# Cross-attention and mixture of experts on one Trainium2 core: attention over context rows as loaded, split products in it, and a new order of work up to the first expert

## What is computed

```
adj = layernorm(x)                       # 4 x 512 x 512, the "adjacency" of a graph attention layer
layer(h, W, a_self, a_neigh, b):         # 8 heads of 64
    feat  = h @ W[head]
    e     = leaky_relu(feat·a_self + (feat·a_neigh)^T, 0.2) - 1e10 * (1 - adj)
    out   = softmax(e) @ feat + b        # concatenated over heads, then elu
x = x + layer(layer(ctx, W0, ...), W1, ...)
xn = layernorm(x)
scores = sigmoid(xn @ router_w^T); top 3 of 8 groups, then top 4 of 32 experts; weights normed, times 2.5
each expert takes at most CAP = 80 tokens: its first ones, in the order of the tokens
x = x + sum over experts of w * (silu(xt @ W_gate) * (xt @ W_up)) @ W_down
      + (silu(xn @ shared_gate^T) * (xn @ shared_up^T)) @ shared_down^T
```

## Time and profile before

| | |
|---|---|
| median of 3 runs | 539.58 us (537.31 to 541.82) |
| span of the profiled execution, first to last instruction | 534.8 us |
| time of the profiled execution itself | not given apart from its span |
| PE matmul busy | 439.8 us, 82% |
| DVE busy | 270.0 us, 50% |
| ACT busy | 159.8 us, 30% |
| DMA | 85.55 MB, mean 160 GB/s |

### The profile page before, as it was taken

How to read it: one execution, slowest core, us unless ns; L and a number is a source line. 1 busy time by engine, 2 the same in 40 slices (tenths; PEclk the granted TensorE clock), 3 DMA queues, 4 the chain that set the end, 5 groups by cost and what they waited for, 6 DMA issues and landing times.

```text
span 534.8 us, 6440 instructions
## 1 busy us (share of the span) xinstructions
PE 439.8 (82%) x2363; PEld 339.8 (64%) x2363; DVE 270.0 (50%) x670; ACT 159.8 (30%) x275; POOL 127.0 (24%) x118
## 2 busy tenths in 40 slices
PE   0251687789958898997999999999999999999920
PEld 0221343334445576876789898888988898888810
DVE  5853638988975999667132243322334334332300
ACT  0222422433187301111112242333324233333220
POOL 0577200300000100000321233332234344332211
PEclk9997679999978999999975999999999999999985
DMA  8687060110126500000178977899979897977250
GB/s 260 162 178 208 25 237 0 79 78 1 80 81 237 198 10 11 0 2 0 39 135 258 277 212 235 249 286 288 319 225 321 256 303 241 307 249 224 28 91 12
DMA packets 41057, 85.55 MB, mean 160 GB/s; under 512 B 14496, under 2 KB 14496, under 8 KB 39488
## 3 DMA queue, kind: packets, MB, share of 16 engines
q1 hardware_dynamic: 32208, 67.74, 37.7%
q0 software_dynamic: 6720, 16.07, 15.1%
q10 hardware_dynamic: 2096, 1.31, 0.8%
HBM read 67.01 MB, written 18.10 MB: 159 GB/s over the span
## 4 chain that ended last, share of the span: by engine, by line
PE 64%; DVE 16%; DMA 7%; issue 5%; ACT 4%; POOL 2%; another core or an unknown queue 1%; ACTq 0%; DVEq 0%; POOLq 0%
PE bank L1266 21%; PE bank L1156 11%; PE bank L1158 10%; PE bank L1157 10%; PE bank L1214 7%; PE bank L1151 4%; DVE bn L846 2%; DMA out_dram<-room 1%; DMA room<-rows_dram,tok 1%; DMA ix<-idx_dram,ixg 1%; DVE xs L905 1%; DMA ctx_buf<-in_ctx_dram,ix 1%; DVE e1r L904 1%; DMA xs<-in_x_dram 1%
## 5 line engine op out<-in xcount | busy, mean ns | idle before, releaser
L1266 PE MATMUL bank<-e1r,ring 128*128 128x80 f32 x1024 | 126.1, 284 | 1.1 <-DVE th L1075 1.1
L1266 PEld LDWEIGHTS bank<-e1r,ring 128*128 128x128 f32 x1024 | 124.9, 202 | 1.3 <-DVE th L1075 1.2
L654 POOL DMA_INDIRECT out_dram<-ctx_buf,tok x32 | 49.2, 1538 | 150.8 <-DMA out_dram<-ctx_buf,tok 73.7
L1075 DVE TENSOR_TENSOR th<-th,bank 128x160 f32<-128x160 f32 (+1 forms) x48 | 21.3, 443 | 125.7 <-ACT th L785 104.6
L1082 DVE TENSOR_TENSOR down<-ring,down 128x1024 fp32r<-128x1024 f32 x32 | 39.2, 1225 | 54.7 <-ACT down L762 54.4
L785 ACT ACTIVATE th<-bank 128x160 f32<-128x160 f32 (+1 forms) x48 | 19.3, 403 | 158.0 <-PE bank L1158 79.5
L1214 PE MATMUL bank<-w,h1T 128*128 128x512 f32 x128 | 58.8, 617 | 5.5 <-DVE sg L899 3.4
L624 POOL DMA_INDIRECT room<-rows_dram,tok x32 | 32.6, 1017 | 90.5 <-ACT tok L672 81.0
L1214 PEld LDWEIGHTS bank<-w,h1T 128*128 128x128 f32 x128 | 24.8, 197 | 37.7 <-issue 29.8
L762 ACT ACTIVATE down<-ring 128x1024 fp32r<-128x1024 f32 x32 | 33.8, 1057 | 32.6 <-PE bank L1158 30.3
L1151 PE MATMUL bank<-ident,ring 128*128 128x128 f32 x48 | 8.5, 336 | 26.9 <-DMA ring<-n_L_ffn_shared_gate_dram 13.0
(11 more groups left out here) (171 smaller groups left out, 728.3 us busy)
## 6 DMA issues: line engine op xcount, KB each, us to landing
ring<-in_L_ffn_W_gate_dram SPq DMA_DIRECT2D x32, 512.0 KB
ring<-in_L_ffn_W_up_dram SPq DMA_DIRECT2D x32, 512.0 KB
ring<-in_L_ffn_W_down_dram SPq DMA_DIRECT2D x32, 512.0 KB
xs<-in_x_dram SPq DMA_DIRECT2D x4, 1024.0 KB, 6.1
out_dram<-xs SPq DMA_DIRECT2D x4, 1024.0 KB, 3.9
out_dram<-room POOLq DMA_DIRECT2D x4, 1024.0 KB, 8.3
rows_dram<-ctx_buf SPq DMA_DIRECT2D x2, 1024.0 KB, 5.3
rows_dram<-h1T SPq DMA_DIRECT2D x2, 1024.0 KB, 4.9
```

The lines of the kernel that those rows point to most:

```text
L654: pool.indirect_dma_start(out=out_rows, out_offset=bass.IndirectOffsetOnAxis(ap=tok[:, n:n + 1], axis=0), in_=ey[:, n % 3, :], in_offset=N ...
L1075: v.tensor_tensor(h, h, up, ALU.mult).then_inc(gu_free, 1)
L1266: last = pe.matmul(bank[2 + i % 2][:, at:at + CAP], w[:, c, P * k:P * k + P], xgT[:, e % 3, c, :], start=(c == 0), stop=(c == KC - 1))
```

## The change

The attention's two layers are applied to all context rows in the order in which they lie in DRAM, and their result f2 (which is elu + 1) is stored to att_dram. Pool then gathers rows of att_dram by idx[idx] and adds them to xs in the DMA. The bias b1 goes into PSUM as a first matmul with a row of ones. Products of both layers are split in high and low parts. elu is made as max(z + 1, min(exp(z), 1)). The maxima and indices of x are taken between the steps of the attention; indices are stored by Pool. The flag is awaited after tile 9 of the second layer, and the check takes sums of squares (ACT, Square) for bn_stats. All orders are written out; the SEL step stands behind D3, MERGE behind S6, the table behind S7, and E0 directly behind the table. Transposes use two PSUM banks all along. Route steps find the chosen entries by match_replace. The 1 that f2 carries too much is taken off again by a bias of -1 in the shared output (`ob`).

```diff
-RING = 3
-XRING = 7
-AHEAD = 5
+RING = 5
+XRING = 5
+AHEAD = 4
+EYS = 2
...
-        att_order = ["W0", "T0", "A0", "W1", "T1", "V0", "A1", "S0", "B0", "T2", "A2", "B1", "T3", "A3", "B2", "B3", "W2", "R0"]
...
-        first_part = [("S", n) for n in range(3)] + [("K", 0), ("S", 3), ("S", 4)] + [("D", n) for n in range(TPG)]
-        first_part += [("S", 5), ("M", 0), ("S", 6), ("S", 7)] + [("D", n) for n in range(TPG, 2 * TPG)] + [("T", 0), ("S", 8), ("S", 9)]
-        shared_rest = [("S", n) for n in (10, 11)] + [("D", n) for n in range(2 * TPG, 3 * TPG)]
+        first_part = [("S", n) for n in range(5)] + [("D", n) for n in range(TPG)]
+        first_part += [("S", n) for n in range(5, 8)]
+        shared_rest = [("D", n) for n in range(TPG, 2 * TPG)] + [("S", n) for n in range(8, 12)] + [("D", n) for n in range(2 * TPG, 3 * TPG)]
...
-            while shared_rest and spent + weight[shared_rest[0][0]] <= total * (e + 1) / EXPERTS:
+            while shared_rest and spent + weight[shared_rest[0][0]] <= total * (e + 1) / (EXPERTS - 3):
...
+            load_ctx(0)
+            load_ctx(1)
+            load_x(0)
+            load_raw(sp, 0)
...
+            load_ctx(2)
+            load_ctx(3)
+            load_x(1)
+            load_raw(sp, 1)
+            load_x(2)
+            load_x(3)
+            load_raw(sp, 2)
...
+            def add_attention(g):
+                pool.wait_ge(idx2_ready[g], 16 * TPG)
...
+                for t in range(TPG * g, TPG * g + TPG):
+                    pool.indirect_dma_start(
+                        out=xs[:, t, :], out_offset=None, in_=att_dram[g],
+                        in_offset=bass.IndirectOffsetOnAxis(ap=ix2[:, t:t + 1], axis=0),
+                        compute_op=ALU.add).then_inc(x1_ready[g], 16)
...
+            for c in range(KC):
+                second_low(c)
+            for g in range(GRAPHS - 1):
+                twice_indexed(g)
+            twice_indexed(3)
+            pool.wait_ge(consts, 3)
+            unless_one_hot(pool, slow_pool)
+            add_attention(0)
+            add_attention(1)
+            add_attention(2)
+            power(0)
+            power(1)
+            add_attention(3)
+            power(2)
+            power(3)
...
+            act.dma_start(b0c[:, :], b0.rearrange("h o -> (h o)").rearrange("(c p) -> p c", p=P),
+                          allow_slow_non_contiguous=True).then_inc(ld_b0, 16)
+            act.dma_start(w_raw[:, KC, :].rearrange("f (h o) -> f h o", h=HEADS),
+                          W0.rearrange("h f o -> f h o")).then_inc(ld_w0, 16)
+            for c in range(KC):
+                act.dma_start(w_raw[:, c, :].rearrange("f (h o) -> f h o", h=HEADS),
+                              W1[:, P * c:P * c + P, :].rearrange("h f o -> f h o")).then_inc(ld_w1, 16)
...
+            act.wait_ge(ld_w1, 16 * KC)
+            for c in range(KC):
+                act.activation(wts[:, HIGH, c, :], w_raw[:, c, :], ACT.Copy).then_inc(w_high, 1)
+            below(0)
+            below(1)
...
+            silu(("S", 0))
+            shared_high(("S", 0))
+            logits(1)
...
+            weights_low(2, 2)
+            weights_low(2, 3)
+            statistics(0)
+            second(14)
+            scales(0)
+            second(15)
+            statistics(1)
+            rows_low(0)
+            scales(1)
+            statistics(2)
+            rows_low(1)
+            scales(2)
+            gated(("S", 0))
+            statistics(3)
+            split(("S", 0), high=False)
+            scales(3)
+            rows_low(2)
...
+                b = out_bank(("B", n))
+                pe.matmul(b[:, :], ones[:, :], b1row[:, :], start=True, stop=False)
+                for c in range(KC):
+                    last = product(b[:, :], lambda h: h1T[g % 2][:, h, c, P * t:P * t + P], lambda h: wts[:, h, c, :],
+                                   start=False, stop=(c == KC - 1))
+                last.then_inc(l2_full, 1)
...
+            second_layer(9)
+            bounds()
+            unless_one_hot(pe, slow_tensor)
+            second_layer(10)
...
+            rows_in(0)
+            router(0)
+            rows_in(1)
+            shared_hidden(0)
+            router(1)
+            rows_in(2)
+            logits_out(0)
+            logits_out(1)
+            shared_hidden(1)
+            router(2)
+            rows_in(3)
+            shared_hidden(2)
+            router(3)
+            logits_out(2)
+            logits_out(3)
+            shared_hidden(3)
+            shared_hidden(4)
+            for n in range(TPG):
+                shared_out(n)
+            selected()
+            shared_hidden(5)
+            shared_hidden(6)
+            merged()
+            shared_hidden(7)
+            tokens()
+            spread(0)
+            for u in mixed_part:
...
```

More of the change, by code:

```diff
@@ new lines, in _ @@
+            act.wait_ge(tp_full, GROUP["CS"] + 1)
+            act.activation(sums[:, :, :], bank[GROUP["CS"] % 2][:, 0:4 * KC].rearrange("p (b n two) -> p b n two", b=2, two=2)[:, :, :, 0],
+                           ACT.Copy).then_inc(tp_free, 1)
+            below(10)
+            hidden_high(8)
+            below(11)
+            hidden_high(9)
+            second(5)
+            exponent(10)
+            exponent(11)
+            ctx_high(3)
+            for t in range(10, 13):
+                square(t)
@@ new lines, in _ @@
+            largest_ctx(0)
+            for t in range(TPG):
+                largest(t)
+            largest_ctx(1)
+            v.wait_ge(w_high, 1)
+            v.tensor_tensor(w0(LOW), w_raw[:, KC, :], w0(HIGH).bitcast(f32), ALU.subtract).then_inc(w0_low, 1)
+            ctx_low(0)
+            ctx_low(1)
+            prepare_bias()
+            place(0)
+            place(1)
+            above(0)
+            above(1)
+            place(2)
+            hidden_low(0)
+            hidden_low(1)
@@ new lines, in _ @@
+            second(1)
+            above(6)
+            above(7)
+            ctx_low(2)
+            largest(6)
+            largest(7)
+            hidden_low(6)
+            second(2)
+            weights_low(1, 2)
+            weights_low(1, 3)
+            hidden_low(7)
+            for t in range(4, 8):
+                place(t)
+            second(3)
+            above(8)
+            above(9)
+            largest(8)
+            largest(9)
+            second(4)
+            hidden_low(8)
@@ new lines, in _ @@
+            hidden_low(9)
+            largest(10)
+            largest(11)
+            second(5)
+            above(10)
+            above(11)
+            ctx_low(3)
+            for t in range(8, 12):
+                place(t)
+            hidden_low(10)
+            second(6)
+            hidden_low(11)
+            low(GROUP["RW"], lambda h: rwT[:, h, :, :], shape=KC, width=KC * EXPERTS)
+            for t in range(12, 16):
+                largest(t)
+            second(7)
+            for t in range(12, 16):
+                place(t)
@@ L1106, in _ @@
             some(routes[0], 99)
[L1107 to L1108 removed]
+            some(routes[1], 2)
+            gated(("S", 4))
+            some(routes[1], 9)
+            split(("S", 4), high=False)
             some(routes[1], 99)
[L1110 to L1115 removed]
+            v.wait_ge(tp_free, GROUP["SEL"] + 1)
+            v.wait_ge(consts, 3 + GRAPHS)
```

1408 lines of the change are left out of this document (791 added, 617 removed).

## The result

The changed kernel takes 558.34 us (557.1 to 559.5, four runs), the kernel before beside it 540.01 (537.31 to 541.82): a ratio of 1.034, 95% interval 1.030 to 1.037. It is slower by 3.4%; 520 was forecast. The changed kernel gave 558.52 in another set, so it hardly varies. So the size of the loss against the kernel before depends on the set, and its sign does not. Nothing here explains the whole of that spread, and therefore the experiments are compared with the changed kernel and with each other.

A forecast was written before the change was run, and what follows sets the result against it. PE saturates only in the expert stretch, so idle PE before E0 is removable. 534.8 − 40 + 4 + 25 − 8.5 = 515.3 us of span, with 4.8 around it 520 us; range 500 to 540.

The forecast's parts named there:

- Stage 3: E0 to the end of E31's hidden product: 231 becomes 256 us, from added S and D units; ring depths cost nothing.
- The rival with ey buffers: Among the experts: two ey buffers bind behind a block add and two Y adds; +12, 532 us; chance 0.07.
- Stage 1: Start to the end of the second layer: 147.0 becomes 107, −40 us, with first-layer activations from 22.
- The pause: Between DMAs on SP's queue, at the start: each lets 394 of ACT's packets pass, so W1 was taken at 20.
- The bound without pauses: Start: W1 goes one for one with SP's 9 MB and lands at 32; +12, 532 us; W1 late had chance 0.16.
- the walk: Going through the written order with unit prices; for stage 1, 22+69+13=104 plus 3 for half clock.
- ACT's two holes: Second layer of the kernel before: ACT holds back uT evacuations for 8.52 and 4.99 us; returning, they cost up to 13.
- Stage 2: End of the second layer to E0: 4 us longer, E0 at 238 instead of 274.1, −36 in total.
- the slower rival: Before E0: accumulating gathers go one after another, last at 169, E0 at 278, 560 us; chance 0.11.
- PE's idle time between D3 and E0: Sign before E0: 25 us or more of idle PE, from SEL, merge, table and first gather.
- Table loads: ACT, Tanh between Silus: six more loads counted as hidden in waits, 2 us for those that are not.
- Stage 4: Tail after E31's hidden product: 21 us against 29.6, −8.5, as D15's block add comes three experts earlier.

The follow-up runs named there:

- experiment 1: Changed kernel with AHEAD = 5 for 4, nothing else: 533.94 us.
- experiment 3: Kernel before with XRING = 5 and AHEAD = 4 for 7 and 5, nothing else of the change: 540.50 us.
- 2: Changed kernel with RING = 3 for 5, testing the rival theory that too many weights are in flight: 560.44 us.
- experiment 4: Changed kernel with SP waiting for W1 before it loads x of the first graph and all that follows: 546.99 us.
- experiment 7: Changed kernel with AHEAD = 5, SP waiting for W1 before x, and DVE's low half of S4 and S7's product and low half moved later: 519.46 us.
- 8: As experiment 7, with D4 and D5 put ahead of the table, D6 and D7 behind it, ahead of the first expert: 508.27 us.
- 9: As 8, with S7 ahead of MERGE, D4 to D7 behind MERGE, S8 between table and first expert: 498.79 us, 0.956 of the kernel before.
- E31: Not a run: an expert of the kernel, as E0 is the first expert; the tail starts at the end of its hidden product.
- Experiment 10: Changed kernel with EXPERTS for EXPERTS - 3 in spreading the shared units, so D15 stands behind E31 again: 555.23 us.

## Why the prediction was wrong, step by step

**Stage 3 (28.2 of the 40 us)** is the step that failed: "Ring 5, XRING 5, AHEAD 4 and two ey buffers change no duration here", argued from PE's 0.2 us of idle time with the old depths. That row says that the old depths sufficed, not that they had slack. A rival was promised for the shallower token ring, but the one that stands there treats the ey buffers alone. What stands behind a moved instruction was asked of Pool's stream, and not of its DMA queue. Experiments 1 and 3 show the cause from both sides, and 2 takes the rival away. The work itself was sized rightly: 256.4 measured with AHEAD = 5. The rival with ey buffers saw a block add that collides with Pool's small transfers, but named the wrong victim (the Y adds, not the gathers) and had 12 us and a chance of 0.07.

Every number was at hand: the earlier trace rows has the block add at 7.84 us, the slots of 5.40 and 11.04. A gather for expert n + 4 is issued behind Y n - 1's add, and wanted ahead of E n + 3, thus after little more than two slots; a D unit's add in between takes eight to ten of these. Slack is worked out from the lead, not from idle time that is absent.

**Stage 1 (8.2).** W1's landing was a term with two bounds, 10 and 32, of which I took 20; 32.2 was measured. The pause that I built on does not exist: SP has issued all its large loads by 10.1, packets of its queue move in every 2 us after that, and the two queues go one for one until 28. The sign that I had named for this step, W1 landing after 28, is the one that came. The bound without pauses was the row at hand (24 to 23 in the earlier trace rows), and I gave it 0.16. Of the Trainium skill, DMA: Bandwidth & Descriptors, "Queues, rings and completion order", I had said that a round-robin by packets of 9 to 17 descriptors would bring W1 sooner; 304 small packets to 302 in experiment 4's first view do not agree with that, and the profile's one for one decides. The rest of the walk was 4 us too slow: with 12 us added for W1 it gives 119, and 115.2 was measured. The wait for the flag (5.0 us) and the first graph's chain came as walked, and ACT's two holes did not return; the trace of experiment 3 lacks them too and has E0 8.3 us earlier, so the 147.0 that I started from had a loss of one execution in it. One sign failed that I had not worked on: first-layer products were to start at 11 to 13 and started at 28.4, since they wait for W0's copy, which stood behind ACT's issue of the loads of W1 until 26.4. It cost nothing here, since the activations wait for W1 until 32.2.

**Stage 2 (3.5).** The gathers behaved as costed: the first graph's are issued from 94.75 and have landed at 108.1 (13.3 us; 6 and 7.8 were taken). The last graph's are late with everything else, as SP's and DVE's timelines show:

```profile
139.32 0.34 SPq L527 DMA_DIRECT2D out_dram<-xs  x1
```

```profile
142.28 0.69 DVE L1216 TENSOR_TENSOR th<-th,bank 128x512 f32<-128x512 f32 x1 [4.92 <-ACT th L901]
```

The store waits for the landing, 139.3, and DVE asks at 142.9, behind the product of S0: hidden by 3.6 us, as forecast 3. So the slower rival gave nearly the measured time, 560, by a mechanism that was not there; a total that fits proves no theory. By steps: from the end of the second layer to the start of SEL's matmuls (202.7) 87.5 us where 82 were walked, to the end of the top-k (225.4) 22.7 where 18 were, the merge to tokf (243.3) 17.9 against 17, and from there to E0 6.4 against 14: together 3.5. The first has PE's wait of 4.7 for the first graph's rows, which I had not: the power step of these rows (asked for at 114.1) stands in Pool's stream behind the issue of twelve gathers, until 116.4. The last was an allowance for half clock and for a gather of 6 us; the first two gathers landed in 3.1 and 2.95.

PE's idle time between D3 and E0 was forecast at 25 us or more. It was 24.1: 2.3 ahead of SEL, 8.6 ahead of MERGE, 9.0 for the table and 4.2 for the first gather. Two of these are the first and the last of the rows below (the middle one is the wait for the later graphs' rows, of which 5.0 in one piece, with 8 in the forecast). The forecast took this idle time as the price of E0's new place, and DVE's two waits of experiment 7 were in its walk. Experiments 7 to 9 show that neither had to be paid.

```profile
PE bank L1442 <- DVE tokf L1419: 9.0, 1, 9.0
PE bank L1442 <- DVE normed L1019: 9.0, 5, 5.0
PE bank L1604 <- DVEq L1250: 8.6, 1, 8.6
```

**Table loads.** Six were counted as hidden and 2 us as visible. There are two in all:

```profile
25.14 1.28 ACT L772 ACT_TABLE_LOAD   x1 [25.14 <-issue]
140.36 1.28 ACT L901 ACT_TABLE_LOAD   x1
```

The four Tanh have no load of their own: the first, at 132.0, comes behind Exp, and the other three behind a Silu. The Trainium skill, ScalarE: Activation LUTs, "Table sets: the hidden batching unit", does list tanh in the set of exp, and the trace agrees; I had quoted its rule without looking at the members. (The 2.66 us for a switch stand in another section of that page, "What ACT_TABLE_LOAD costs"; each load here took 1.28.)

**Stage 4.** 21.4 measured, 21 forecast: luck. The forecast's path has no waits for tokens among the experts, and in the runs that come near to it, experiments 1 and 9, the tail is 25.6 and 25.8. There Pool issues three Y adds, 4.6 to 4.8 us apart, after E31's end (in 1 at 510.22, 514.80 and 519.43), where the walk counted two. The 21.4 came about because the adds caught up while PE stood in the waits of stage 3. Experiment 10's 8.5 is measured against that shortened tail; against the 25.6 of experiment 1 its 29.9 is only 4.3 more. So the term was some 4 us too good for the kernel that I had in mind, and what D15's new place costs elsewhere was not asked.

## What to carry to other kernels

A ring that is made shallower is costed by its lead: slots between issue and use, against the largest transfer that can stand ahead in the same DMA queue. That PE never waited with the deeper ring says nothing on it. And when the unit that everything waits for is moved forward, keep the filling work around it: idle time ahead of it was worth 21 us here in the two steps of experiments 8 and 9, and the waits of 2 us and more that remained among the experts also cost half clock behind them.

## What had not been expected of the hardware

ACT's sequencer stood 23.25 us in issuing four DMAs of 1024 small packets each, while the same took 5.83 us with SP's queue quiet (experiment 4). For that time ACT does nothing else: its copy of W0 began at 26.4. A DMA issue is not free for an engine that has work to do.

After a gap of 2.6 to 6.2 us PE ran at the lower clock level: E products of 3.57 us took 6.8. At E0, behind gaps of 9.0 and 4.2, the clock was 0.50 for 16.3 us:

```profile
249.70:266.00 16.30, 16.30 (x75) 15.82 (x75) 1.78 (x6) 1.48 (x4) 0.84 (x1) 0.50 0.32 108
```

In the three places of stage 3 that doubled the price of each wait: 14.0 us of waiting, 27.8 lost against experiment 1.
